# Five of a tile's split products handed to TensorE whole: a DLRM tower with a compressed interaction network on one core

## The reference, cut to what matters

```python
e = jnp.stack([tbl_0[ids[:, 0]], ..., tbl_31[ids[:, 31]]], axis=1)   # (1024, 32, 16)
x0 = h = e
for i in range(3):
    z = (x0[:, :, None, :] * h[:, None, :, :]).reshape(B, F * G, E)
    y = relu(einsum('oc,bce->boe', W[i], z) + b[i][None, :, None])   # 128 outputs
    x_keep, h = (y[:, :64], y[:, 64:]) if i < 2 else (y, y)
    xs.append(x_keep)
z = sum(concatenate(xs, axis=1), axis=2)                             # (1024, 256)
h = maximum(concatenate([z, dense_ctx], axis=1) @ W_top1 + b_top1, 0)
h = maximum(h @ W_top2 + b_top2, 0)
y = h @ W_top3
```

## Time and profile before

| | |
|---|---|
| median of 3 runs | 1115.0 us (1112.32 to 1119.09) |
| span of the profiled execution, first to last instruction | 1109.1 us |
| what lies around the span | the three runs' times are 3.2 to 10.0 us above it, the median 5.9 us |
| mean granted clock of TensorE | 0.960 of 2.4 GHz |
| TensorE (PE) | 994.0 us busy, 90% |
| VectorE (DVE) | 987.2 us busy, 89% |
| GpSimd (POOL) | 882.4 us busy, 80% |
| ScalarE (ACT) | 572.7 us busy, 52% |
| HBM read | 181.15 MB, 166 GB/s over the span |

### The profile page before, as it was taken

The page is one execution under the profiler, slowest core; times in us unless marked ns, Lnnn a source line. Parts: engine busy times, 40 slices in busy tenths (PEclk is TensorE's granted clock), DMA queues, the critical chain, the costliest instruction groups (busy, mean ns, idle before and its releaser), DMA issues.

```text
span 1109.1 us, 12343 instructions
## 1 busy us (share of the span) xinstructions
PE 994.0 (90%) x3281; PEld 611.0 (55%) x3281; DVE 987.2 (89%) x842; ACT 572.7 (52%) x683; POOL 882.4 (80%) x525
## 2 busy tenths in 40 slices
PE   3167989998997979999899989999899999999988
PEld 2134556564654646555556656555556656565665
DVE  6246999999996999999999999999999999999982
ACT  0234556554654545565555645565455556555553
POOL 7645899997977979997999979997999966665760
PEclk9588999998998999999899999999899999999999
DMA  6199989899886869898888879888788989888500
GB/s 118 14 195 198 184 170 190 195 186 191 168 192 133 164 163 199 175 194 177 168 183 182 195 174 193 184 186 190 156 182 179 192 194 191 185 197 193 124 1 1
DMA packets 111813, 184.55 MB, mean 166 GB/s; under 512 B 19570, under 2 KB 24178, under 8 KB 111540
## 3 DMA queue, kind: packets, MB, share of 16 engines
q1 hardware_dynamic: 103604, 182.24, 76.8%
q0 software_dynamic: 8192, 2.11, 1.9%
HBM read 181.15 MB, written 3.15 MB: 166 GB/s over the span
## 4 chain that ended last, share of the span: by engine, by line
POOL 29%; DVE 18%; issue 18%; DMA 15%; PE 13%; ACT 4%; SPq 2%; DVEq 1%; POOLq 0%; ACTq 0%
POOL low L490 15%; POOL looked_up L480 12%; DVE unsplit L1043 9%; DMA xcols<-xrows 6%; PE y L604 6%; DMA shifted<-xcols 5%; DVE prod L1043 4%; PE y L612 4%; PE y L627 2%; POOL tail_parts L498 2%; DMA spread<-xcols 1%; SPq L390 1%; DMA looked_up<-in_tbl,ids_now 1%; ACT h L794 1%; DVE tail L1025 1%
## 5 line engine op out<-in xcount | busy, mean ns | idle before, releaser
L490 POOL TENSOR_TENSOR low<-unsplit,high 128x1024 fp32r<-128x1024 f32 x222 | 543.7, 2454 | 110.5 <-ACT high L808 108.3
L808 ACT CAST high<-unsplit 128x1024 fp32r<-128x1024 f32 x320 | 334.0, 1047 | 330.2 <-DVE unsplit L1043 322.7
L604 PE MATMUL y<-prod,w1T 128*128 128x512 f32 x1024 | 491.4, 609 | 5.1 <-ACT kept L800 2.7
L480 POOL DMA_INDIRECT looked_up<-in_tbl,ids_now x256 | 291.3, 1138 | 69.3 <-issue 58.6
L1043 DVE TENSOR_TENSOR prod<-spread,h 128x1024 f32<-128x1024 f32 x256 | 307.1, 1210 | 7.9 <-ACT h L794 7.4
L1043 DVE TENSOR_TENSOR unsplit<-spread,h 128x1024 f32<-128x1024 f32 x256 | 307.7, 1212 | 4.2 <-ACT h L794 4.2
L604 PEld LDWEIGHTS y<-prod,w1T 128*128 128x128 f32 x1024 | 196.0, 195 | 171.1 <-issue 149.5
L627 PE MATMUL y<-low,w2T_high 128*128 128x512 f32 x512 | 222.5, 518 | 48.4 <-POOL low L490 47.5
L612 PE MATMUL y<-high,w2T_high 128*128 128x512 f32 x512 | 217.1, 424 | 5.7 <-ACT high L808 5.5
L1051 DVE TENSOR_TENSOR low<-unsplit,high 128x1024 fp32r<-128x1024 f32 x98 | 187.3, 1911 | 22.3 <-ACT high L808 22.3
L612 PE MATMUL y<-high,w2T_low 128*128 128x512 f32 x512 | 202.9, 396 | 0.0
(11 more groups left out here) (114 smaller groups left out, 482.4 us busy)
## 6 DMA issues: line engine op xcount, KB each, us to landing
spread<-xcols SPq DMA_DIRECT2D x256, 512.0 KB, 6.9
shifted<-xcols SPq DMA_DIRECT2D x124, 256.0 KB, 4.6
shifted_tail<-xcols SPq DMA_DIRECT2D x124, 64.0 KB, 4.9
looked_up<-in_tbl,ids_now POOLq DMA_INDIRECT x256
xcols<-xrows SPq DMA_DIRECT2D x32, 96.0 KB, 5.5
spread<-in_L_rec_W SPq DMA_DIRECT2D x3, 512.0 KB, 7.1
spread<-in_L_rec_W SPq DMA_DIRECT2D x1, 1024.0 KB, 10.9
wt<-in_W_top SPq DMA_DIRECT2D x2, 512.0 KB, 9.4
```

Of the source, the lines that this page charges most:

```text
L480: pool.indirect_dma_start(out=looked_up[:, f, :], out_offset=None, in_=tables[f][:, :], in_offset=bass.IndirectOffsetOnAxis(ap=ids_now[:, ...
L490: pool.tensor_tensor(low[kind][r][:, :, :], unsplit[kind][r][:, :, :], high[kind][r][:, :, :].bitcast(F32), ALU.subtract).then_inc(s_low[k ...
L604: last = pe.matmul(y[:, :], w1T[:, ITEM * n + c, :], z[:, c, :], start=(n == 0 and c == 0), stop=(item == LAST1 and c == ITEM - 1))
L808: act.copy(high[kind][r][:, :, :], unsplit[kind][r][:, :, :]).then_inc(s_high[kind], 1)
```

## The change

The four full chunks of layer 0 (both its items) and item (2, 6) become WHOLE. Their products go to `prod` (a ring of 4, now for 11 items of a tile and not 8), PE multiplies them with fp32 weights (`w0T`, `w2T_whole`), and their casts on ACT and low parts on DVE are gone. Seven items of layer 2 stay with ACT and POOL, and POOL's order is the same but for the last slot, where (2, 6) also becomes WHOLE and one low part is gone. In the preparation one cast and one subtraction of 128x512 go, and one copy of 128x256 comes.

```diff
-SPLIT2_BY_DVE = [(2, 6)]
+WHOLE2 = (2, 6)
...
 def kind_of(item, last):
-    if item[0] == 1:
+    if item[0] < 2 or item == WHOLE2:
         return WHOLE
-    return BY_DVE if item[0] == 0 or item in (LAST_BY_DVE if last else SPLIT2_BY_DVE) else BY_POOL
+    return BY_DVE if last and item in LAST_BY_DVE else BY_POOL
...
-        w0T_high = sb("w0T_high", [P, GROUP, P], F32R)
-        w0T_low = sb("w0T_low", [P, GROUP, P], F32R)
+        w0T = sb("w0T", [P, GROUP, P])
...
+        w2T_whole = sb("w2T_whole", [P, ITEM, P])
...
-                    pe.wait_ge(s_made[BY_DVE], plan.entry(after(t, -2), LAST0) + 1)
+                    pe.wait_ge(s_made[WHOLE], plan.entry(after(t, -2), LAST0) + 1)
...
                     for c in range(ITEM):
-                        last = pe.matmul(y[:, :], w1T[:, ITEM * n + c, :], z[:, c, :], start=(n == 0 and c == 0),
-                                         stop=(item == LAST1 and c == ITEM - 1))
+                        w = w2T_whole[:, c, :] if layer == 2 else (w0T, w1T)[layer][:, ITEM * n + c, :]
+                        last = pe.matmul(y[:, :], w, z[:, c, :], start=(n == 0 and c == 0),
+                                         stop=(item in (LAST0, LAST1) and c == ITEM - 1))
...
-                act.wait_ge(s_used[BY_DVE], plan.entry(s, LAST0) + 1)
+                act.wait_ge(s_used[WHOLE], plan.entry(s, LAST0) + 1)
...
+                    if WHOLE2[1] // (GROUP // ITEM) == n - 2 - GROUPS:
+                        of = ITEM * WHOLE2[1] % GROUP
+                        dve.tensor_copy(w2T_whole[:, :, :], source[:, of:of + ITEM, :])
```

More of the change, by code:

```diff
@@ L441, in _ @@
             load_spread((BLOCKS - 1, START + 1), GROUPS - 1)
-            sp.wait_ge(s_made[BY_DVE], plan.entry((BLOCKS - 1, TILES_PER_BLOCK - 2), LAST0) + 1)
+            sp.wait_ge(s_made[WHOLE], plan.entry((BLOCKS - 1, TILES_PER_BLOCK - 2), LAST0) + 1)
             sp.dma_start(wt1[:, :].rearrange("p (c n) -> p c n", n=TOP1),
@@ L610, in multiply @@
                     for c in range(ITEM):
-                        for w in ((w0T_high, w0T_low) if layer == 0 else (w2T_high, w2T_low)):
+                        for w in (w2T_high, w2T_low):
                             pe.matmul(y[:, :], w[:, ITEM * n + c, :], z[:, c, :],
-                                      start=(n == 0 and c == 0 and w in (w0T_high, w2T_high)), stop=False)
+                                      start=(n == 0 and c == 0 and w is w2T_high), stop=False)
             def multiply_low(s, item):
@@ L626, in multiply_low @@
                 for c in range(ITEM):
-                    last = pe.matmul(accumulator(s, layer)[:, :], (w0T_high if layer == 0 else w2T_high)[:, ITEM * n + c, :],
-                                     z[:, c, :], start=False, stop=(item in (LAST0, LAST2) and c == ITEM - 1))
+                    last = pe.matmul(accumulator(s, layer)[:, :], w2T_high[:, ITEM * n + c, :],
+                                     z[:, c, :], start=False, stop=(item == LAST2 and c == ITEM - 1))
                 last.then_inc(s_used[kind], 1)
@@ L952, in _ @@
                             once.unsqueeze(1).to_broadcast([P, GROUP - 1, FIELDS])).then_inc(s_sym, 1)
-            homes = [w0T_high[:, :, :], w0T_tail[:, :]]
+            homes = [w0T[:, :, :], w0T_tail[:, :]]
             homes += [w1T[:, GROUP * g:GROUP * (g + 1), :] for g in range(GROUPS)]
             homes += [w2T_high[:, GROUP * g:GROUP * (g + 1), :] for g in range(GROUPS)]
-            lows = {0: w0T_low[:, :, :]}
-            lows.update({2 + GROUPS + g: w2T_low[:, GROUP * g:GROUP * (g + 1), :] for g in range(GROUPS)})
+            lows = {2 + GROUPS + g: w2T_low[:, GROUP * g:GROUP * (g + 1), :] for g in range(GROUPS)}
             for n, home in enumerate(homes):
```

## The result

The changed kernel took 1104.4 us (1102.65 to 1105.12, four runs) against 1117.1 of the kernel before on the same chip: a ratio of 0.9876, 95% interval 0.984 to 0.9911. It is 12.7 us faster, where 21 were forecast. Its profiled execution took 1104.9 us and has a span of 1103.1 us; in all later runs the time stands 1.8 to 2.2 us above the span. Differences of a few us between the two profiles are not the change's alone. Lines have moved by up to three: L605 are whole products, L613 and L628 high and low ones, L1046 the multiplication, L1077 the addition to `acc_kept` (L1074 before).

The account below looks back on a forecast made before the run. No single bound by averages: PE and DVE both near 90%; PE would set ordinary slots. A block takes 88.4 + 32.7 = 121.1 us, 3.5 less; six give 21, so span 1088 plus 5.9 is 1094 us, range 1080 to 1114.

Parts of the forecast that it names:

- I take the row's 1.72: On PE, each of three items made whole costs 1.72 us in place of 1.40; a slot needs 29.4 us.
- The rival of 1.86 us for an item: On PE, four passes of 0.2325 us make a whole item 1.86 us: 0.42 more per slot, 1107 us; chance 0.03.
- The lock on the lookups: In the first slot, a lookup on POOL takes 1.77 us behind DVE's low part, others 0.97; 0.8 us comes back.
- The low part of (2, 2) one slot earlier: On POOL, the slot before the first: this low part, 18.4 us behind the transposes, starts 1.8 us earlier; bounds nothing and 3.4.
- the sums: DVE's remaining work besides 18 multiplications at 1.13 us; together about 24 us a slot.
- What DVE gives, PE takes: In a block's three ordinary slots, PE sets the pace: 88.4 us in place of 88.5.
- A quarter of the 3.7: In the first slot, PE's slow clock after the wait still costs 0.9 us of the 3.7 lost around it before.
- The chain of x: Rival: transposes through `shifted`, (0, 0) and (2, 2) bound every slot; 30.4 us for an ordinary one, 1134 us; chance 0.09.
- Start and end at zero: Preparation (under 1 us less) and the last two slots (PE 0.32 us more each) taken as zero; bounds -1 and +1 us.

Follow-up runs that it names:

- the same two table entries: Addition behind (2, 0) and lookups two at a time from (2, 1) on: 1158.1 us on the kernel before, 1079.1 us on the changed kernel.

## Why the prediction was right in sign and short in size

- **PE.** "I take the row's 1.72": right. Undisturbed slots are 29.31 us against 29.4 forecast. The rival of 1.86 us for an item would have made them 29.8 or more; the window of 29.40 with PE busy throughout, and all ordinary slots of the kernel with the addition moved, speak against it. The slots of 29.9 look like it by chance. The Trainium skill, "FP8 and Floating Point Precision", section "TensorE Precision Notes", counts four passes for true FP32 and gives no time for one. The price of 0.2325 us a pass came from the split rows, and that is what the runs deny: a fourth of a whole product's 0.86 us is 0.215.
- **The lock on the lookups.** "0.8 us of POOL's time come back": right. The last lookup has 0.97, none has 1.77, and the group's mean is 973 ns against 1138 before.
- **"The low part of (2, 2) one slot earlier ... I take 1.8 us earlier."** This step failed in three blocks of six, the one shown among them. The term counted DVE's work by the engine's own durations and had POOL's low parts of (2, 0) and (2, 1) at 14.1 us as if nothing on DVE depended on them. The addition and the copy to `acc_kept`, folded into "the sums", are caught between them. POOL's (2, 2) came at 19.0 in place of 16.6 and `emb` at 14.4 in place of 11.3, of which 1.2 is the longer transfer. With the addition moved, 16.6 is met exactly, and so it is in the two blocks where nothing was caught ahead of the first slot.
- **"What DVE gives, PE takes", 29.5 for an ordinary slot.** Right for half the blocks, wrong for the others, for the same reason: 29.7 to 29.9. DVE's busy time missed by 40 us: 20 are the additions (64.4 for 44.2), 7 the copies (19.3 for 12.8), and 5 the three low parts of the last slot, which the forecast had left out; 8 are not traced.
- **"A quarter of the 3.7" for the clock.** Wrong in the good direction, and luck: in the slot shown, waits of 1.50 and 2.05 us left the clock at 1.00. That offset the larger waits. The 33.6 us are 29.3 and 4.3 around the waits, against 29.4, 2.4 and 0.9 in the forecast, and the first slots without a pause, 31.2 to 33.6 and 35.1 once, average 33.0 against 32.7. The rows do not say when the clock falls: in the first slot of the first block the waits are 1.45 and 2.03 us, and behind them the granted clock was 0.50:

```profile
153.00:155.00 2.00, 2.00 (x4) 1.01 (x3) 0.52 (x1) 0.00 (x0) 1.67 (x3) 0.50 1.06 202
```

- **The chain of x.** `shifted` holds no ordinary slot, so the rival was rightly held unlikely. But its path from (0, 0) on is the one that binds. From transposes to (0, 0) it is 13.0 to 13.3 us in the 29.3 slots and 15.7 in the 29.9 ones. The prediction put the limit at 15.2, and 0.5 beyond it gives its 29.4 + 0.5. DVE is never idle ahead of (0, 0) in these slots: the caught addition makes it late, not the transfer.
- **Start and end at zero.** The end is equal (229.7 us behind the last of the six blocks, 229.8 before). The start is 3.6 us longer in this profile. Three variants of the kernel before, with the same preparation, have 125.5 to 126.4 us where its own profile has 122.0, so this is no price of the change that these profiles can show.

What became of the gain, from the profiles: the six blocks took 747.7 us, where 757.2 less 21 makes 736. Of the 11.5 missing, the ordinary slots hold 4.6 (535.0 without pauses, against 6 x 88.4), the first slots 2.0, and the rest, about 5, is a second pause of the lookups (below), which this profile of before did not have. The first two go with the lock, as moving the addition shows. Whether the pause belongs to the kernel or to the execution stays open: both profiles of the changed kernel have it (5.72 and 5.64 us), and the one of before is of an execution faster than all of its four runs. Moving the addition gives 18 us, more than these 6.6. It also takes four first slots to 30.7 to 31.4, below the forecast (the first block's stays at 34.9), and in its profile the two slots with a pause are 2.4 and 3.0 us shorter; how much of that is chance is open.

That the tenth of a microsecond decides between 1.9 and 4.34 was read and not tried by itself. It holds in all fourteen profiles: 52 additions meet a pair with the cast at 1.34 to 2.09 us and take over 4 us, 132 meet one with the cast at 2.17 to 2.61 and take under 2.

## What to carry to other kernels

When work is taken off an engine that shares something with another, ask what its remaining instructions of the same kind will now overlap: the removed ones had also set the phase. An instruction with two SBUF inputs belongs where the other engine has a gap, and a row of back-to-back instructions on the other engine is a wait for all of them. And once a change has made an engine slack, try again the orders that were bad before: the same two table entries cost 41 us without this change and gave 25 with it.

## What the runs showed of the hardware that was not expected

- **The lock is not handed over between back-to-back instructions.** A DVE operation on 128x512 with two SBUF inputs takes 0.68 us alone, 1.9 when it gets in behind one POOL low part, 4.34 behind two, and a 128x1024 one (1.21 alone) up to 6.5. Multiplications with one input in PSUM stay at 1.21 throughout. The Trainium skill, "SBUF — State Buffer", section "Who interferes with whom", says that whoever issues first holds the shared pair for the whole instruction; the runs agree for two instructions that meet, and add that POOL keeps it over the next one too if that is ready in time. A lookup counts here: in the kernel before, a DVE low part at 313.42 starts 0.36 us into one, with POOL's next low part right behind, and takes 4.08 us. The same section infers that a tensor_tensor does not stop descriptor generation; the runs contradict it. In the kernel before, 53 of the 70 lookups that start during a DVE tensor_tensor with two SBUF inputs take over 1.4 us, and 2 of the other 186 do; with DVE's low parts gone, so are the lookups of 1.77.
- **A pause in the lookups.** In every profile the 114th indirect transfer is issued late, and in ten of fourteen the 227th, another 113 later. In the changed kernel:

```profile
334.51 0.95 POOL L480 DMA_INDIRECT looked_up<-in_tbl,ids_now  x1 [9.09 <-issue]
...
776.71 0.96 POOL L480 DMA_INDIRECT looked_up<-in_tbl,ids_now  x1 [5.72 <-issue]
```

  Before, it was 8.73 and 0.35 us; in the other profiles 4.5 to 9.2, and at the second place from 0.2 to 5.7. The slots at 309.93 and 744.95 are 38.7 and 39.1 us long by it. It is the same count of transfers in each kernel, while the time of the 114th goes from 329 to 354 us. Nothing was tried on it, and the cause stays open.
